# An FFN stream in 24 two-tile sets over both token halves, with seven block products in place of eight in 19 of them

## What is computed

```python
hidden_i = x @ wi.T + 2*common_i(x) + 2*expert_lora_i(x)      # 256 -> 1024
hidden_o = relu(hidden_i) @ wo.T + 2*common_o + 2*expert_lora_o   # 1024 -> 256
probs = softmax(hidden_states.mean(axis=1) @ gate_w)          # per sequence
top_w, top_i = top_k(probs, 2); top_w = top_w / top_w.sum()
out = sum_e combine[e] * (gelu(hidden @ w1[e] + b1[e]) @ w2[e] + b2[e])
return x + out
```

## Time and profile before

| what | value |
|---|---|
| median of 3 executions | 285.5 us (284.98 to 285.66) |
| profiled execution | 285.79 us, span of the trace 284.0 us |
| TensorE busy | 277.7 us, 98% of the span |
| VectorE (DVE) busy | 154.2 us, 54% |
| ScalarE (ACT) busy | 108.2 us, 38% |
| GpSimd (POOL) busy | 19.8 us, 7% |
| matmuls in the main stream | 1152 of 1227 |

### The profile page before, as it was taken

The page is one execution under the profiler, slowest core; times in us unless marked ns, Lnnn a source line. Parts: engine busy times, 40 slices in busy tenths (PEclk is TensorE's granted clock), DMA queues, the critical chain, the costliest instruction groups (busy, mean ns, idle before and its releaser), DMA issues.

```text
span 284.0 us, 3387 instructions
## 1 busy us (share of the span) xinstructions
PE 277.7 (98%) x1227; PEld 225.3 (79%) x1227; DVE 154.2 (54%) x278; ACT 108.2 (38%) x169; POOL 19.8 (7%) x26
## 2 busy tenths in 40 slices
PE   8989999999999999999999999999999999999994
PEld 3658888888888888888888888888888888888883
DVE  1686568454646556877656344667343445434433
ACT  3455555335236346834442224434222122221220
POOL 1244520303000000000000000000000000000000
PEclk9999999999999999999999999999999999999999
DMA  5993000000461320172241000000100000200002
GB/s 166 289 332 81 2 1 3 0 0 0 153 218 42 108 76 0 49 249 76 78 143 74 3 0 0 0 2 35 39 1 2 0 0 0 76 0 0 0 2 74
DMA packets 11776, 16.89 MB, mean 59 GB/s; under 512 B 1584, under 2 KB 7920, under 8 KB 11760
## 3 DMA queue, kind: packets, MB, share of 16 engines
q1 hardware_dynamic: 11056, 15.89, 17.6%
q10 hardware_dynamic: 704, 0.79, 0.9%
HBM read 14.58 MB, written 2.10 MB: 59 GB/s over the span
## 4 chain that ended last, share of the span: by engine, by line
PE 92%; DMA 3%; SPq 1%; DVE 1%; issue 1%; ACT 1%; DVEq 0%
PE out_ps L480 15%; PE out_ps L484 15%; PE out_ps L481 15%; PE hid_ps L480 15%; PE hid_ps L481 15%; PE hid_ps L484 15%; DMA lora_raw<-in_lora 3%; PE spare_ps L566 1%; SPq L277 1%; SPq L286 0%; DVE x_sb L772 0%; PE spare_ps L500 0%; ACT w_hi L399 0%; PE spare_ps L495 0%; DVE w_lo L625 0%
## 5 line engine op out<-in xcount | busy, mean ns | idle before, releaser
L412 ACT ACTIVATE hid<-hid_ps,bias_sb 128x512 f32<-128x512 f32 x64 | 44.2, 690 | 112.1 <-PE hid_ps L484 112.1
L480 PE MATMUL out_ps<-hid_hi,w_hi 128*128 128x512 f32 x192 | 74.8, 390 | 0.8 <-DVE hid_lo L640 0.8
L480 PE MATMUL hid_ps<-act_hi,w_hi 128*128 128x512 f32 x192 | 75.2, 392 | 0.0
L481 PE MATMUL hid_ps<-act_lo,w_hi 128*128 128x512 f32 x192 | 74.8, 390 | 0.0
L484 PE MATMUL hid_ps<-act_hi,w_lo 128*128 128x512 f32 x192 | 74.7, 389 | 0.0
L481 PE MATMUL out_ps<-hid_lo,w_hi 128*128 128x512 f32 x192 | 74.7, 389 | 0.0
L484 PE MATMUL out_ps<-hid_hi,w_lo 128*128 128x512 f32 x192 | 74.7, 389 | 0.0
L643 DVE CAST hid_hi<-hid 128x512 fp32r<-128x512 f32 x64 | 27.3, 426 | 76.5 <-ACT hid L412 76.4
L645 DVE TENSOR_TENSOR hid_lo<-hid,hid_hi 128x512 fp32r<-128x512 f32 x64 | 44.3, 693 | 2.2
L480 PEld LDWEIGHTS out_ps<-hid_hi,w_hi 128*128 128x128 f32 x192 | 36.0, 188 | 8.7 <-DVE hid_lo L640 1.2
L484 PEld LDWEIGHTS hid_ps<-act_hi,w_lo 128*128 128x128 f32 x192 | 36.1, 188 | 7.5
(11 more groups left out here) (55 smaller groups left out, 110.3 us busy)
## 6 DMA issues: line engine op xcount, KB each, us to landing
stage<-in_w SPq DMA_DIRECT2D x16, 512.0 KB, 3.4
x_sb<-in_xT SPq DMA_DIRECT2D x3, 512.0 KB, 12.0
outT<-x_sb SPq DMA_DIRECT2D x6, 256.0 KB, 2.1
lora_raw<-in_lora SPq DMA_DIRECT2D x6, 192.0 KB, 9.0
stage<-in_woT SPq DMA_DIRECT2D x2, 512.0 KB, 9.2
lora_raw<-in_lora SPq DMA_DIRECT2D x2, 288.0 KB, 8.5
stage<-in_wiT SPq DMA_DIRECT2D x1, 512.0 KB, 9.5
x_sb<-in_xT ACTq DMA_DIRECT2D x1, 256.0 KB, 4.2
```

The costliest lines, as they stand in the source:

```text
L412: eng.activation(hid[:, s % 2, :], hid_ps[:, s % NH, :], ACT.Gelu, bias=bias_sb[:, b, k, f:f + 1]).then_inc(s_hid, 1)
L480: eng.matmul(out, w_h, a_h, start=start, stop=False)
L481: eng.matmul(out, w_h, a_l, start=False, stop=False)
```

## The change

The stream becomes 24 sets. A set is two f tiles by both token halves of one sequence, so four hidden tiles in four PSUM banks; the stages are the conditional network for sequence 0 and 1 (sets 0 to 3 and 4 to 7), then for each sequence its two experts (sets 8 to 23). In a set, the four up tiles are four sums of two block products, a 2 by 2 by 2 product of blocks. Sets 0, 1, 2, 3 and 8 (PLAIN) take the eight products; the other 19 take seven, in the Winograd form of Strassen's scheme. A product is three matmuls as before. The seven need sums of weight blocks (S1 to S4, `weight_sums` on POOL), sums of token tiles (T1 to T4, `token_sum` on POOL) with their high and low parts (`sum_high` on ACT, `sum_low` on DVE), a copy of m1 (`first_copy` on ACT), two running sums (`second_sum`, `third_sum`) and three sums into tiles (`tile_sum`) on DVE. The down side keeps its six matmuls for each hidden tile. The downs of a set are issued between the ups of the next.

All weights are now streamed, one set at a time through three buffers on either side: the conditional ones are loaded, multiplied with factors, merged (`merge_up`, `merge_down` on DVE) and split again for each sequence and set. The split of the low part moves to POOL (`up_low`, `down_low`), of the high part to ACT (`up_high`, 1024 columns in a set of seven; `down_high`, 512). For the experts, Gelu is applied in place in PSUM, and `hid_high` (ACT) and `hid_low` (DVE) then scale by the mixing weight. The conditional output is kept in `y_sb` and split again as raw tiles (`raw_high`, `raw_low`).

```diff
-            for s in range(N_STEP):
-                up(s)
-                if s >= LAG:
-                    down(s - LAG)
-                for n in PRODUCTS_AT.get(s, ()):
-                    lora_product(n)
-                if s in ROUTE_AT:
-                    router_logits(ROUTE_AT[s])
+    PLAIN = (0, 1, 2, 3, 8)
+    SEVEN_TILES = [(0, 0), (1, 1), (1, 0), (0, 1)]
+    SEVEN = ["m1", "m6", "m2", "m7", "m5", "m4", "m3"]
+    OPERANDS = {"m1": (0, 0), "m2": (2, 2), "m3": (S4, 3), "m4": (3, T4), "m5": (S1, T1), "m6": (S2, T2),
+                "m7": (S3, T3)}
+    RAW_HI_AT = {1: [(0, 0)], 2: [(0, 1)], 5: [(1, 0), (1, 1)], 10: [(2, 0)], 12: [(2, 1)]}
+    SUM_HI_AT = {2: [(0, 0)], 3: [(0, 1)], 7: [(1, 0)], 8: [(1, 1)], 13: [(2, 0)], 14: [(2, 1)]}
+    LORA_HI_AT = {1: [(1, 0)], 2: [(1, 1), (1, 2)], 3: [(1, 3), (1, 4)]}
...
+            def bank_free(q, bank):
+                if q:
+                    eng.wait_ge(s_hid_lo, 4 * (q - 1) + bank + 1)
+                if bank == 0 and q >= 1 and ("d", q) in PRODUCTS:
+                    eng.wait_ge(s_merge, product_count("d", q))
...
+            for q in range(1, NSET):
+                operands(q)
+                if seven(q):
+                    one_of_seven(q, "m1", 0, True)
+                    one_of_seven(q, "m6", 1, True)
+                    down(q - 1, 0)
+                    next_up_factor(q)
+                    eng.wait_ge(s_r1, sevens_before(q) + 1)
+                    one_of_seven(q, "m2", 0, False)
+                    one_of_seven(q, "m7", 2, True)
+                    down(q - 1, 1)
+                    one_of_seven(q, "m5", 3, True)
+                    eng.wait_ge(s_r3, sevens_before(q) + 1)
+                    one_of_seven(q, "m4", 2, False)
+                    router_logits(q)
+                    down(q - 1, 2)
+                    next_down_factor(q)
+                    eng.wait_ge(s_add, 3 * sevens_before(q) + 1)
+                    one_of_seven(q, "m3", 3, False)
+                    down(q - 1, 3)
+                else:
+                    plain_tile(q, 0)
+                    down(q - 1, 0)
+                    next_up_factor(q)
+                    plain_tile(q, 1)
+                    down(q - 1, 1)
+                    plain_tile(q, 2)
+                    down(q - 1, 2)
+                    next_down_factor(q)
+                    plain_tile(q, 3)
+                    down(q - 1, 3)
...
+            def hid_high(q, j):
+                if q:
+                    eng.wait_ge(s_down, 4 * (q - 1) + j + 1)
...
+            def slot_c(q):
+                if q in LOGITS_AT:
+                    router_start(LOGITS_AT[q])
+                for b, lot in LORA_LO_AT.get(q, ()):
+                    lora_low(b, lot)
+                for p, m in SUM_LO_AT.get(q, ()):
+                    sum_low(p, m)
...
+            for q in range(1, NSET):
+                if seven(q):
+                    second_sum(q)
+                hid_low(q - 1, 3)
+                if q + 2 < N_COND:
+                    merge_up(q + 2, hid_ps[:, 3, :])
+                slot_a(q)
+                if seven(q):
+                    third_sum(q)
+                hid_low(q, 0)
+                slot_b(q)
+                if seven(q):
+                    tile_sum(q, 1)
+                    tile_sum(q, 2)
+                if cond(q):
+                    hid_low(q, 1)
+                    slot_c(q)
+                    if q + 1 < N_COND:
+                        merge_down(q + 1, hid_ps[:, 0, :])
+                else:
+                    slot_c(q)
+                    hid_low(q, 1)
+                if seven(q):
+                    tile_sum(q, 3)
+                hid_low(q, 2)
```

More of the change, by code:

```diff
@@ L275, in _ @@
+        program = ctx.enter_context(nc.Block())
+        @program.sync
         def _(eng):
@@ new lines, in _ @@
+            eng.memset(zeros, 0.0).then_inc(s_zero, 1)
+            x0_low(0, 0)
+            lora_low(0, 0)
+            x0_low(1, 0)
+            merge0(0)
+            merge0(1)
+            up0_low(0)
+            up0_low(1)
+            lora_low(0, 2)
+            x0_low(0, 1)
+            x0_low(1, 1)
+            merge_up(1, out_ps[:, 2, :])
+            hid_low(0, 0)
+            merge_down(0, out_ps[:, 3, :])
+            hid_low(0, 1)
+            merge_up(2, out_ps[:, 0, :])
+            hid_low(0, 2)
@@ new lines, in _ @@
+            hid_low(NSET - 1, 3)
+            for n, (kd, t, cols) in enumerate(FINAL):
+                at = half(NB - 1, t).start
+                mine = slice(at + cols.start, at + cols.stop)
+                eng.wait_ge(s_done, ENDS.index((kd, t)) + 1)
+                eng.scalar_tensor_tensor(out=x_sb[:, kd, mine], in0=out_ps[:, kd * NT + t, cols],
+                                         scalar=mixed_b2[:, NB - 1, 1, kd:kd + 1], in1=x_sb[:, kd, mine],
+                                         op0=ALU.add, op1=ALU.add).then_inc(s_final, 1)
@@ L805 @@
         "woT": t(a["L0_cond_wo"]),
-        "lora": lora,
+        "lora": np.concatenate(lots, axis=2),
         "gate": a["L0_ffn_gate_w"],
```

1159 lines of the change are left out of this document (667 added, 492 removed).

## The result

The changed kernel takes 309.79 us (median of 4 runs, 308.16 to 311.20) against 285.58 us (284.98 to 285.89) for the kernel before on the same chip: a ratio of 1.0849, with a 95% interval of 1.0792 to 1.0905. It is 8.5% slower. The profiled execution took 308.16 us, with a span of 306.2.

The account below looks back on a forecast made before the run. TensorE was taken as the bound: 252.2 us of work from a 10.5 us start, with tail and offset, gave 268.3 + S; S = 18.6 gave 286.9, less 0.3 to the median: 286.6 us, range 282.0 to 291.5.

Parts of the forecast that it names:

- the forecast itself: Whole kernel: S between 16.6 and 20.3 us, time 284.6 to 288.3 us, likeliest 286.6; chance 0.4.
- the line to "no change": Measured time: above 286.4 us counts as slower, below 284.6 as faster.
- S: TensorE's stalls over the stream: summed to 18.6 us, 15.5 without port contention, 20.3 with the most of it.
- The point of balance: Whole kernel: the change pays only if TensorE's stalls stay below 17.5 us, against 2.7 before.
- The clock: TensorE's clock falls in the long waits, costing 2.4 us once, or again in set 0: 289 to 291.4 us; chance 0.2.
- the forecast's own wait of 5 us: Set 3, before set 4: TensorE waits 4.3 us for DVE's `merge_down`, with 0.7 for port contention: 5.0.
- The price of the lock: POOL's `up_low` delaying DVE's `lora_low` at the shared port: 0.7 us in sets 2 and 3, 0.5 in set 1.
- The rival of a steady set that doesn't close: Sets of seven products overrun by 0.3 us each, 5.7 us over 19 sets: 292 us; chance 0.08.
- The rival of stalls below the balance: Sets 0 to 3: ACT's copies issue closer and DVE keeps the port, S = 14, median 282.0 us; chance 0.32.

Follow-up runs that it names:

- the last version: Changed kernel with early and late sets reordered, later waits moved by order, and DVE's four last token-sum splits together in set 14: 275.31 us, ratio 0.9643.
- the version with S = 13.0: Changed kernel with only the order of work changed, in both the early sets and the sets from 5 on: 281.45 us, ratio 0.9877 to the kernel before.
- the filler run: Changed kernel with 15 and 25 matmuls, whose results are overwritten, put on TensorE ahead of sets 3 and 4: 305.37 us.
- the late order: Changed kernel with only order changed from set 5 on: router parts and activation splits behind `hid_low` of tile 2, token sums of set 6 after the picks: 294.12 us.

## Why the prediction was wrong

The predicted time was 286.6 us, in a range that ended at 291.5; the median is 309.8. The direction was the likelier one given, at 0.5, but little is owed to it: the forecast itself was only 0.2 us past the line to "no change", and the loss is 24.2 us. The frame held: work 252.2 us, a start at 10.56 (10.5), a steady set at 10.20, and a profiled time of 268.3 + S. With S = 40.0 that gives 308.3 for 308.16 measured, and with the 7.4 of the last version 275.7 for 275.31. The point of balance, S = 17.5, held too: the version with S = 13.0 is faster than before. The step that failed is the sum of stalls, 40.0 for 18.6, in three of its terms: the clock behind the waits, put at nothing in it, took 7.3; POOL's hold on DVE was priced at 0.7 us in sets 2 and 3, where it cost 1.7; and beside the router and the `raw_low` of sets 6, 11 and 12 it was put at 0.5 or at nothing, where most of another 7.8 us went (2.9 in set 6 and 4.9 in sets 11 to 13, clock aside).

| Term of S | predicted | after | last version |
|---|---|---|---|
| set 0 | 4.1 | 4.1 | 1.4 |
| sets 1, 2 | 3.6 | 6.6 | 1.4 |
| set 3 (with the wait before set 4) | 5.0 | 7.7 | 1.2 |
| set 4 | 0 | 2.9 | 0.5 |
| set 5 | 0.5 | 1.2 | 1.3 |
| set 6 | 1.9 | 6.5 | 0.2 |
| set 8 | 1.55 | 1.7 | 0 |
| sets 11 to 13 | 1.9 | 6.8 | 0.3 |
| others | 0 | 2.5 | 1.1 |
| sum | 18.6 | 40.0 | 7.4 |

Each is the set's length less 0.2267 us a matmul, 0.24 for each pair of factor products in it and 0.2 for a router.

**The clock** was a rival at 0.2 that would cost 2.4 us once, or twice with set 0. It came true in four sets, with 7.3 of the 21.4 us missing; the filler run took 3.9 of it away and nothing else. The error was to hold it for another case beside the forecast, when it follows from the forecast's own wait of 5 us. The Trainium skill's warning of idle gaps between bursts of matmuls ("TensorE: Matmul & The Clock Gate", Why this matters for your kernels) was cited there as not shown by any run; this trace shows it, with 0.79 granted in set 4.

**The price of the lock** was taken as 0.5 to 0.7 us a set, and looked for in sets 1 to 3 alone. The earlier trace rows had shown that a blocked instruction takes what is left of POOL's, and I let that happen to the four `lora_low` once, or twice for 1.3. It happened twice, and cost 1.7 us in each of sets 2 and 3 (3.41 and 3.40 for 1.76). The rule of the Trainium skill ("SBUF — State Buffer", SBUF: two separate sides), that the port pair is held for the whole instruction, agrees with the rows shown, and would have been the better price than my middle value. In set 6 I added 0.5 for one POOL instruction beside `raw_low` and costed the router's instructions at 0.15 to 0.23 us beside four token sums; three of them took 1.0 and the two `raw_low` 2.90 for 1.25 (at the 2.50 of four `sum_low`, of the same form), so that 4.61 us of wait stood where 1.1 was predicted. Holding the token sums back gave 3.5 of that back. In set 11 two `raw_low` took 3.32, and in set 12 L938, L952 and L953 took 0.88 to 1.18 us each before a wait of 2.38. The prediction had 1.9 us for sets 11 to 13, but from ACT's table loads and undisturbed router steps. There the lock is read from the durations; the late order removed the waits, and no run moved POOL's work alone in these two sets.

**Put at nothing** were also sets 7, 9, 14, 15, 17 and 20, with 2.5 us in all (of sets 14 to 17 it said that their extra work fits in the spare 1 us); they were not looked into one by one.

**Right were** the places: the wait of 4 to 6 us before set 4 released by `merge_down`, the one at the first router, 1.7 in set 8, 4.1 in set 0. The rival of a steady set that doesn't close is refuted: 45 matmuls in 10.20 us. The rival of stalls below the balance (S = 14) named a state that can be reached, but by another order and not by this one.

**Open.** Why a wait of the same length lowers the clock in one execution and not in another isn't settled. Nor is what the remaining 1.4 us in each of sets 0 and 1 would take. Set 8 with seven products wasn't tried.

## What to carry to other kernels

When a change takes work from the bounding engine and gives it to helpers with room to spare on average, cost it at the borders: write down each helper's queue in order, from the operand that the bounding engine waits for backwards, and take out of it whatever isn't needed there. Here the arithmetic saved 12.9 us of matmuls, and order alone, with the lock and the clock that follow from it, was worth 34.5 (309.8 against 275.3). Where DVE and POOL both work out of SBUF, price each DVE instruction beside a POOL one at what is left of POOL's, however small the first is (the reductions and the instructions fed from PSUM kept their times here), and keep long POOL work out of a chain of small dependent DVE steps. And once a wait of some microseconds on TensorE is forecast, half-clock matmuls behind it belong in the same case.
